# The bias of a transformer block's first FFN product moved out of the weights and into ScalarE's Relu, with a second ScalarE pass over h, and a head worked by pairs of tiles

## Chip, core and metric

The kernel runs on one core of one Trainium2 chip. The metric is the device time of one execution in microseconds (us); the median of several runs counts. The core's engines run side by side, each through its own instructions in order: TensorE (PE in the rows, PEld for its weight loads), VectorE (DVE), ScalarE (ACT), GpSimd (POOL) and SyncE (SP), which issues most transfers. They are kept in step by semaphores: an instruction that waits holds up everything behind it on its engine.

## What is computed

For x of 8 batches x 1024 tokens x 256 channels, in fp32:

```python
xn = (x - mean) / sqrt(var + 1e-5)
q, k, v = split(xn @ qkv_w + qkv_b)            # 16 heads of 16
q, k = l2norm(q), l2norm(k)                    # per head
kv = einsum('bhnd,bhne->bhde', k, v)
attn = einsum('bhnd,bhde->bhne', q, kv) @ proj_w + proj_b
ffn = relu(xn @ W1 + b1) @ W2 + b2             # 256 -> 1024 -> 256
out = x + attn + ffn
```

The last two lines' products are most of the work. b1 is not zero.

## The kernel before

**Precision.** Each operand of a product is split into a high part in fp32r and the rest, a low part; a product is three matmuls (`product`: high x high, high x low, low x high). A high part is a ScalarE copy with rounding, a low part a VectorE (or GpSimd) subtraction of the high part.

**Tiling.** A batch is two halves s (u = 0, 1) of 512 tokens, 4 tiles of 128. W1's 1024 columns are 8 chunks j. `ffn_up(s, u, j)` makes chunk j of W1^T xn^T in PSUM bank `w_bank[j % 2]` with 6 matmuls of 512 columns; `h_high` (ScalarE, L540) writes `h_hi = Relu(w_bank)`; `h_low` (VectorE, L843) writes `h_lo = max(w_bank, 0) - h_hi`; `ffn_down` multiplies both with W2. TensorE's order is written out by hand: `ffn_up` of chunk j + 2, `ffn_down` of chunk j, and between them the query and key products `query_key` (banks `v_bank`, evacuated by `qk_out`, L518 and L475), `gather` (xn^T k into `g_bank`), `key_value`, `project` and, at the end of a batch, `attend`. `ffn_up` of chunk j + 2 waits for `h_lo` of chunk j, since they share a bank. `attend` waits for `m_lo`, the low part of the projected key-value matrix, a VectorE instruction that stands behind `h_low` of the next half's chunk 0 and the norms of the next half's q and k. `gather` waits for `k_lo`. The first `ffn_down` of a half waits for `yT_out` (L555), which empties `o_bank`.

**How the bias of layer 1 gets in.** Channel 0 of xn is raised by 1 for every token (`xn[:, :, 0:1] + 1`). Then xn_raised @ W gives xn @ W + W[0], so each weight matrix gets its bias in row 0's stead by adding (bias - W[0]) to *every row*: that works because a normalised row sums to 0, so that adding the same c to all 256 rows adds c times the raised 1 only. For W1 the row c = b1 - W1[0] is spread over 128 partitions by small fp32 matmuls (`raise_by`, with `raise_signs` made by GpSimd and `raise_rows` cleared by VectorE and loaded by ScalarE's queue), and VectorE adds it to the weights in four parts (`raise_w1`, L769), before `w1_high` and `w1_low` split them. qkv_w is raised in the same way by rows that are loaded spread out.

**The opening.** Half 0 has no predecessor. VectorE takes statistics, `normalise_first` writes the four tiles of xn (L761) and raises channel 0 (L765), TensorE transposes all four (`transpose_x`, 8 transposes), ScalarE and VectorE split each of two banks (`xT_high_first`, `xT_low_first`), and `ffn_up_first` makes chunk 0. The orders of batch 0 and of the first half of batch 1's preparations are written out in `opening` for every engine. In later halves xn^T is made by VectorE's 32x32 transposes and 16 transfers each from SP's queue; q^T too.

**The end.** The last half's result stays token-major. GpSimd adds the output bias to the loaded x (`add_last_bias`, L377) early in batch 7; `bias_out` was loaded and summed in the opening. In the last half `attend(b, 0, w_bank)` waits for the `h_lo` of chunk 7.

Of the kernel before, what the change touches and what calls it, by code (L numbers as in the profile page):

```python
# [62 lines left out]
def build(nc, x, qkv_w, qkv_b, proj_w, proj_b, w1, b1, w2, b2, out):  # L63
# [6 lines left out]
    with ctx:  # L70
# [14 lines left out]

        w1_hi, w1_lo = (sb(f"w1_{n}", [P, KC, INTER], F32R) for n in ("hi", "lo"))
# [21 lines left out]
        h_hi, h_lo = (sb(f"h_{n}", [P, RING, HALF], F32R) for n in ("hi", "lo"))  # L108
        qk_even = sb("qk_even", [P, TILES, 2 * C])
# [22 lines left out]
        bias_ffn = kv[:].rearrange("p g n -> p (g n)")  # L132
# [3 lines left out]
        raise_rows = qk_sq[:].rearrange("p t n -> p (t n)")  # L136
# [15 lines left out]
        w1_raise = [g_bank[:, 0:2 * P], kv_bank[:, 0:2 * P], v_bank[1][:, 0:2 * P], v_bank[1][:, 2 * P:4 * P]]  # L152
# [14 lines left out]
        w1_raise_ready, qkv_raise_ready = sem("w1_raise_ready"), sem("qkv_raise_ready")  # L167
        qkv_rows_loaded = sem("qkv_rows_loaded")
        signs_set, warm_set, raise_rows_cleared = sem("signs_set"), sem("warm_set"), sem("raise_rows_cleared")
        w1_raised, w1_hi_ready, w1_ready = (sem(f"w1_{n}") for n in ("raised", "hi_ready", "lo_ready"))  # L170
# [9 lines left out]
        xn_done, xn_hi_done, xn_split_done = sem("xn_done"), sem("xn_hi_done"), sem("xn_split_done")  # L180
        last_y_set = sem("last_y_set")
# [13 lines left out]
        h_ready, h_done, h_lo_done = (sem(n) for n in ("h_ready", "h_done", "h_lo_done"))  # L195
# [67 lines left out]
        def _(sp):  # L263
# [60 lines left out]
            sp.dma_start(bias_out[:], proj_b.partition_broadcast(P)).then_inc(bias_o_loaded, 16)  # L324
            sp.dma_start(bias_ffn[:], b2.partition_broadcast(P)).then_inc(bias_o_loaded, 16)
# [7 lines left out]
            def half(b, s, u, last):  # L333
# [31 lines left out]
        def _(pool):  # L365
# [37 lines left out]
            nc.gpsimd.memset(raise_signs[:], 0.0).then_inc(signs_set, 1)  # L403
# [637 lines left out]
        def _(pe):  # L1041
# [6 lines left out]
            def tile(t):  # L1048
                return slice(t * P, (t + 1) * P)
# [247 lines left out]
```

## Time and profile before

| | |
|---|---|
| median of 3 runs | 568.85 us (568.74 to 569.23) |
| profiled execution, its own time | 569.29 us |
| its span, first to last instruction | 567.5 us |
| mean granted TensorE clock | 0.998 |
| busy: PE / DVE / ACT / POOL | 559.3 / 414.4 / 282.4 / 119.9 us |
| waits of PE by name (longest) | 1.3 us in all for xn in the head; 0.9 or less each else |

The busy times are those of one execution. A row of the timeline gives start, duration, engine, line, operation, what is written and read, how many instructions, and in brackets how long the engine idled before it and what released it. Matmuls overlap, so a busy PE says little; the distance between the starts of matmuls says more (512 columns: 0.23 us, 256 columns: 0.12 us when nothing waits).

### The profile page before, as it was taken

What the parts mean: (1) busy time and instruction counts of PE and PEld (TensorE: products, weight loads), DVE (VectorE), ACT (ScalarE), POOL (GpSimd) and SP (SyncE); (2) the same over time, 40 slices, a digit from 0 to 9 for tenths busy, and PEclk for the clock granted to TensorE, in tenths of its full rate; (3) what the DMA queues carried; (4) which work ended last, traced back from release to release, by engine and by line L of the source; (5) the groups of instructions that cost most, each with busy time, mean ns of one, the idle gap of its engine ahead of it and who ended that gap; (6) DMA issues with size and microseconds to landing.
All of it is one profiled execution on the core that took longest, in us unless ns stands there. A gap on an engine that the chain in (4) does not pass through costs nothing.

```text
span 567.5 us, 8956 instructions
## 1 busy us (share of the span) xinstructions
PE 559.3 (99%) x2722; PEld 475.5 (84%) x2722; DVE 414.4 (73%) x807; ACT 282.4 (50%) x516; POOL 119.9 (21%) x148
## 2 busy tenths in 40 slices
PE   7999999999999999999999999999999999999997
PEld 6788887888888888888888888888888888888896
DVE  6887887777786767958678585776778767683755
ACT  3586473655435563365634556445554555433421
POOL 2532422502052020520204202231024300150100
PEclk9999999999999999999999999999999999999999
DMA  8322136353523535035451353425444252424423
GB/s 297 112 81 50 29 80 97 81 100 72 101 28 86 95 85 98 16 86 94 85 89 25 85 94 85 81 34 103 76 90 67 43 102 41 82 31 75 110 38 75
DMA packets 141398, 45.36 MB, mean 80 GB/s; under 512 B 133314, under 2 KB 136386, under 8 KB 141380
## 3 DMA queue, kind: packets, MB, share of 16 engines
q1 hardware_dynamic: 139264, 44.61, 39.0%
q10 hardware_dynamic: 2116, 0.53, 0.6%
q8 instruction: 9, 0.15, 0.1%
q14 instruction: 9, 0.07, 0.0%
HBM read 20.98 MB, written 8.39 MB: 52 GB/s over the span
## 4 chain that ended last, share of the span: by engine, by line
PE 89%; SPq 4%; DVE 2%; ACT 2%; issue 1%; DMA 1%; ACTq 0%; DVEq 0%
PE o_bank L1044 11%; PE o_bank L1045 11%; PE o_bank L1046 11%; PE w_bank L1046 10%; PE w_bank L1044 10%; PE w_bank L1045 10%; PE v_bank L1044 6%; PE v_bank L1045 6%; PE v_bank L1046 6%; SPq L308 3%; PE g_bank L1046 3%; PE g_bank L1045 3%; PE g_bank L1044 3%; PE kv_bank L1165 1%; DMA x_sb<-x 1%
## 5 line engine op out<-in xcount | busy, mean ns | idle before, releaser
L843 DVE SCALAR_TENSOR_TENSOR h_lo<-w_bank,h_hi 128x512 fp32r<-128x512 f32 x128 | 87.5, 683 | 34.1 <-ACT h_hi L540 32.6
L540 ACT ACTIVATE h_hi<-w_bank 128x512 fp32r<-128x512 f32 x128 | 76.4, 597 | 70.6 <-PE w_bank L1046 68.8
L1046 PE MATMUL w_bank<-xT_hi,w_lo 128*128 128x512 f32 x254 | 100.0, 394 | 0.0
L1044 PE MATMUL w_bank<-xT_hi,w_hi 128*128 128x512 f32 x254 | 99.7, 393 | 0.0
L1045 PE MATMUL w_bank<-xT_lo,w_hi 128*128 128x512 f32 x254 | 99.7, 393 | 0.0
L1044 PE MATMUL o_bank<-h_hi,w_hi 128*128 128x512 f32 x240 | 95.0, 396 | 0.3 <-ACT wvp_raw L555 0.3
L1045 PE MATMUL o_bank<-h_lo,w_hi 128*128 128x512 f32 x240 | 94.7, 395 | 0.0
L1046 PE MATMUL o_bank<-h_hi,w_lo 128*128 128x512 f32 x240 | 94.6, 394 | 0.0
L372 POOL TENSOR_TENSOR xn_lo<-xn,xn_hi 128x256 fp32r<-128x256 f32 x56 | 41.6, 742 | 224.4 <-ACT xn_hi L475 215.9
L387 POOL TENSOR_TENSOR y_sb<-y_sb,y_rows 128x256 f32<-128x256 f32 x56 | 53.4, 959 | 130.6 <-DVE y_rows L882 108.1
L518 ACT ACTIVATE qk_sq<-v_bank 128x512 f32<-128x512 f32 x64 | 38.4, 599 | 79.0 <-PE v_bank L1046 78.6
L810 DVE TENSOR_REDUCE qk_v<-qk_sq 128x32 f32<-128x512 f32 x64 | 43.4, 680 | 35.6 <-ACT qk_sq L518 35.6
L1046 PEld LDWEIGHTS w_bank<-xT_hi,w_lo 128*128 128x128 f32 x254 | 47.7, 188 | 10.2
L1044 PEld LDWEIGHTS w_bank<-xT_hi,w_hi 128*128 128x128 f32 x254 | 47.7, 188 | 9.6 <-DVE w_lo L702 0.6
L1045 PEld LDWEIGHTS w_bank<-xT_lo,w_hi 128*128 128x128 f32 x254 | 47.7, 188 | 9.4
L1044 PEld LDWEIGHTS o_bank<-h_hi,w_hi 128*128 128x128 f32 x240 | 46.5, 194 | 10.1 <-ACT wvp_raw L555 0.7
L1045 PEld LDWEIGHTS o_bank<-h_lo,w_hi 128*128 128x128 f32 x240 | 46.9, 195 | 9.4
L1046 PEld LDWEIGHTS o_bank<-h_hi,w_lo 128*128 128x128 f32 x240 | 46.7, 195 | 9.2
L1044 PE MATMUL v_bank<-wqk_hi,xT_hi 128*128 128x512 f32 x128 | 50.3, 393 | 0.1
L1045 PE MATMUL v_bank<-wqk_lo,xT_hi 128*128 128x512 f32 x128 | 50.3, 393 | 0.0
L1046 PE MATMUL v_bank<-wqk_hi,xT_lo 128*128 128x512 f32 x128 | 50.1, 391 | 0.0
L493 ACT ACTIVATE xn<-x_sb,ln_offset,ln_rstd 128x256 f32<-128x256 f32 x52 | 27.0, 590 | 29.4 <-DVE ln_offset L754 29.4
(188 smaller groups left out, 986.3 us busy)
## 6 DMA issues: line engine op xcount, KB each, us to landing
qT_lo<-blocks SPq DMA_DIRECT2D x256, 32.0 KB, 1.9
x_sb<-x SPq DMA_DIRECT2D x15, 512.0 KB, 3.9
y_sb<-x SPq DMA_DIRECT2D x60, 128.0 KB, 3.5
out<-y_sb SPq DMA_DIRECT2D x58, 128.0 KB, 2.7
xT_raw<-blocks SPq DMA_DIRECT2D x224, 32.0 KB, 1.9
y_sb<-w SPq DMA_DIRECT2D x4, 256.0 KB, 4.8
w_raw<-w SPq DMA_DIRECT2D x1, 768.0 KB, 8.8
x_sb<-x SPq DMA_DIRECT2D x2, 256.0 KB, 2.9
```

The lines of the kernel that those rows point to most:

```text
L308: sp.dma_start(to_pairs[j * BLOCK:(j + 1) * BLOCK, :, g * run:(g + 1) * run], by_row[g * BLOCK:(g + 1) * BLOCK, j]).then_inc(moved, 16)
L372: nc.gpsimd.tensor_tensor(xn_lo[:, u, t, :], xn_of(s)[:, t, :], xn_hi[:, u, t, :].bitcast(F32), ALU.subtract).then_inc(xn_split_done, 1)
L387: nc.gpsimd.tensor_tensor(y_sb[:, u, t, :], y_sb[:, u, t, :], y_rows[:, u, t, :], ALU.add).then_inc(y_done, 1)
L493: done = nc.scalar.activation(to[:, t, :], x_sb[:, u, t, :], ACT.Identity, bias=ln_offset[:, t:t + 1], scale=ln_rstd[:, t:t + 1])
L518: nc.scalar.activation(qk_sq[:, t % 2, :], v_bank[t % 2][:], ACT.Square).then_inc(qk_sq_done, 1)
L540: nc.scalar.activation(h_hi[:, j % RING, :], w_bank[j % 2][:], ACT.Relu).then_inc(h_done, 1)
L810: nc.vector.tensor_reduce(qk_v[:, t, :], qk_sq[:, t % 2, :].rearrange("p (h d) -> p h d", d=D), AXIS.X, ALU.add).then_inc(qk_ss_done, 1)
L843: nc.vector.scalar_tensor_tensor(h_lo[:, r, :], w_bank[j % 2][:], 0.0, h_hi[:, r, :].bitcast(F32), ALU.max, ALU.subtract).then_inc(h_lo_do ...
L1044: nc.tensor.matmul(to, left[0], right[0], start=first, stop=False, skip_group_check=shared)
L1045: nc.tensor.matmul(to, left[0], right[1], start=False, stop=False, skip_group_check=shared)
L1046: return nc.tensor.matmul(to, left[1], right[0], start=False, stop=last, skip_group_check=shared)
L1165: nc.tensor.matmul(kv_raw[:, g, :, :], wv_hi[:, k, heads], g_parts[:, k, :, heads], start=g == 0 and k == 0, stop=False, skip_group_check= ...
```

## The change

1. W1 is split as loaded: no `raise_by` for W1, no `raise_signs`, no `raise_rows`, no `raise_w1`. xn stays raised by 1 in channel 0. So TensorE's `w_bank` now holds xn @ W1 + W1[0]. With c = W1[0] - b1, h = Relu(w_bank - c).
2. ScalarE's Relu takes the bias `c_up = -c` as a column per partition, and gives `h_hi`. A second ScalarE pass, after a wait for the first, writes `h_g = h_hi + c` (`c_down = c`) in fp32. VectorE then writes `h_lo = max(w_bank, c) - h_g`, which is h - h_hi.
3. c is made once: b1 and W1[0] are loaded as 8 rows of 128, GpSimd subtracts, TensorE transposes to 128x8, ScalarE writes `c_up` and `c_down`.
4. The head: `normalise_first` raises and signals each pair of tiles; `transpose_pair`, `xT_high_pair`, `xT_low_pair` work by pairs (256 columns), `ffn_up_first` now makes chunks 0 and 1, in 24 matmuls of 256 columns. W1's chunk 0 is split first, ahead of ScalarE's square root and VectorE's normalisation.
5. `bias_out` is now loaded and summed in the last batch, into free parts of x_sb: two transfers on SP's queue ahead of `load_y`, one GpSimd addition ahead of `add_last_bias`.

```diff
             def h_high(s, j):
 
+                r = j % RING
+                if is_first(s) and j == 0:
+                    act.wait_ge(c_set, 2)
                 wait(act, h_ready, JC * s + j + 1)
-                nc.scalar.activation(h_hi[:, j % RING, :], w_bank[j % 2][:], ACT.Relu).then_inc(h_done, 1)
+                nc.scalar.activation(h_hi[:, r, :], w_bank[j % 2][:], ACT.Relu, bias=c_up[:, j:j + 1]).then_inc(h_done, 1)
+                wait(act, h_done, JC * s + j + 1)
+                nc.scalar.activation(h_g[:, j % 2, :], h_hi[:, r, :].bitcast(F32), ACT.Identity,
+                                     bias=c_down[:, j:j + 1]).then_inc(h_less_c, 1)
...
             def h_low(s, j):
                 r = j % RING
-                wait(dve, h_done, JC * s + j + 1)
-                nc.vector.scalar_tensor_tensor(h_lo[:, r, :], w_bank[j % 2][:], 0.0, h_hi[:, r, :].bitcast(F32),
-                                               ALU.max, ALU.subtract).then_inc(h_lo_done, 1)
+                wait(dve, h_less_c, JC * s + j + 1)
+                nc.vector.scalar_tensor_tensor(h_lo[:, r, :], w_bank[j % 2][:], c_down[:, j:j + 1],
+                                               h_g[:, j % 2, :], ALU.max, ALU.subtract).then_inc(h_lo_done, 1)
...
@@ ScalarE's opening @@
-            act.wait_ge(raise_rows_cleared, 1)
-            for row, of_w1 in enumerate((b1.rearrange("(o n) -> o n", o=1), w1[0:1, :])):
-                act.dma_start(raise_rows[row:row + 1, :], of_w1).then_inc(rows_loaded, 16)
+            for n, row in enumerate((b1, w1[0:1, :].rearrange("o n -> (o n)"))):
+                act.dma_start(c_rows[:, n, :], row.rearrange("(j p) -> j p", p=P)).then_inc(rows_loaded, 16)
             act.wait_ge(const_set, 2)
             nc.scalar.activation(unread[:], positive[:], ACT.Sqrt)
+            w1_high_first()
             ln_sqrt(0)
-            xT_high_first(0, 0, 0)
             w1_high(0)
-            xT_high_first(0, 0, 1)
+            w1_high(1)
+            xT_high_pair(0, 0)
+            xT_high_pair(0, 1)
+            xT_high_pair(1, 0)
+            xT_high_pair(1, 1)
+            act.wait_ge(c_ready, 1)
+            nc.scalar.activation(c_up[:], c_in_bank, ACT.Identity, scale=-1.0).then_inc(c_set, 1)
+            copy(c_down[:], c_in_bank).then_inc(c_set, 1)
+            w2_high(0)
             h_high(0, 0)
-            w1_high(1)
-            w2_high(0)
...
@@ VectorE's opening @@
-            nc.vector.memset(raise_rows, 0.0).then_inc(raise_rows_cleared, 1)
             variance(0, 0, 0)
+            w1_low_first()
             normalise_first()
-            raise_w1(0)
-            xT_low_first(0, 0, 0)
             w1_low(0)
-            xT_low_first(0, 0, 1)
-            raise_w1(1)
+            for a in range(PAIRS):
+                for k in range(KC):
+                    xT_low_pair(a, k)
+            w1_low(1)
             h_low(0, 0)
-            w1_low(1)
 
             def opening():
                 h_low(0, 1)
-                raise_w1(2)
-                raise_w1(3)
                 w1_low(2)
                 h_low(0, 2)
...
@@ TensorE's opening @@
-            keep_warm(14)
-            pe.wait_ge(signs_set, 3)
-            pe.wait_ge(rows_loaded, 32)
-            raise_by(w1_raise[0], 0).then_inc(w1_raise_ready, 1)
+            keep_warm(13)
+            pe.wait_ge(const_set, 4)
+            pe.wait_ge(c_rows_done, 1)
+            nc.tensor.transpose(c_in_bank, c_rows[:, 0, :], ident[0:JC, 0:JC]).then_inc(c_ready, 1)
             keep_warm(2)
-            pe.wait_ge(const_set, 4)
-            transpose_x(0, 0)
-            raise_by(w1_raise[1], 2 * P).then_inc(w1_raise_ready, 1)
+            transpose_pair(0)
+            transpose_pair(1)
             ffn_up_first()
-            ffn_up(0, 0, 1)
-            raise_by(v_bank[1][:], 4 * P).then_inc(w1_raise_ready, 1)
...
@@ SyncE, a half of a batch @@
+                if last and u == 0:
+                    sp.wait_ge(xn_done, s + 1)
+                    sp.dma_start(bias_out, proj_b.partition_broadcast(P)).then_inc(bias_o_loaded, 16)
+                    sp.dma_start(bias_ffn, b2.partition_broadcast(P)).then_inc(bias_o_loaded, 16)
```

## Rows read from the trace of the kernel before

**Rows 1.** The page's busy times: engine, us, share, instructions.
```profile
PE 559.3 (99%) x2722; PEld 475.5 (84%) x2722; DVE 414.4 (73%) x807; ACT 282.4 (50%) x516; POOL 119.9 (21%) x148
```
**Rows 2.** Windows, one steady batch: stretch, length, busy by engine, PEclk, DMA share, GB/s.
```profile
349.87:418.30 68.43, 68.43 (x327) 58.03 (x327) 50.20 (x100) 35.12 (x65) 13.51 (x16) 1.00 0.40 77
```
**Rows 3.** Groups by shape on ACT, one steady batch: busy us, mean ns, idle before.
```profile
L540 ACT ACTIVATE h_hi<-w_bank 128x512 fp32r<-128x512 f32 x16 | 9.5, 597 | 8.5 <-PE w_bank L1046 8.5
...
L555 ACT ACTIVATE xn_first<-o_bank,bias_T 128x512 f32<-128x512 f32 x2 | 1.4, 688 | 0.2 <-PE o_bank L1046 0.2
```
**Rows 4.** Timeline of ACT, steady batch: a wait on its own result.
```profile
379.01 2.08 ACT L493 ACTIVATE xn<-x_sb,ln_offset,ln_rstd 128x256 f32<-128x256 f32 x4 [2.16 <-DVE ln_offset L754]
381.12 0.21 ACT L497 ACTIVATE xn<-xn 128x4 f32<-128x4 f32 x1
```
**Rows 5.** The chain that ended last, around 28.6 us: start, us, what.
```profile
28.63 0.48 ACT h_hi L540
```
**Rows 6.** Timeline and landing time of W1's first part, the head.
```profile
L270 SPq DMA_DIRECT2D y_sb<-w x1: 434/434/434, 1.7 to 1.7; - x1
...
DMA to landing us min/median/max: 3.8/3.8/3.8
...
7.13 1.38 DVE L761 TENSOR_SCALAR xn<-x_sb,ln_mean,ln_rstd 128x256 f32<-128x256 f32 x4
...
13.00 0.60 ACT L540 ACTIVATE h_hi<-w_bank 128x512 fp32r<-128x512 f32 x1 [1.81 <-PE w_bank L1105]
...
14.97 0.19 PEld L1044 LDWEIGHTS w_bank<-xT_hi,w_hi 128*128 128x128 f32 x1 [0.60 <-DVE w_lo L702]
```
**Rows 7.** Timeline of PEld: query product of tile 2, batch 0.
```profile
30.14 0.20 PEld L1044 LDWEIGHTS v_bank<-wqk_hi,xT_hi 128*128 128x128 f32 x1 [0.35 <-ACT qk_even L475]
```
**Rows 8.** Timelines of DVE and PEld, rest of batch 0, in pairs.
```profile
58.52 0.69 DVE L843 SCALAR_TENSOR_TENSOR h_lo<-w_bank,h_hi 128x512 fp32r<-128x512 f32 x1
...
59.29 0.19 PEld L1044 LDWEIGHTS w_bank<-xT_hi,w_hi 128*128 128x128 f32 x1
...
73.47 0.69 DVE L843 SCALAR_TENSOR_TENSOR h_lo<-w_bank,h_hi 128x512 fp32r<-128x512 f32 x1 [0.27 <-ACT h_hi L540]
...
74.26 0.19 PEld L1044 LDWEIGHTS w_bank<-xT_hi,w_hi 128*128 128x128 f32 x1
...
85.07 0.69 DVE L702 TENSOR_TENSOR m_lo<-g_bank,m_hi 128x512 fp32r<-128x512 f32 x1
...
85.83 0.20 PEld L1044 LDWEIGHTS v_bank<-qT_hi,m_hi 128*128 128x128 f32 x1 [1.26 <-issue]
...
93.34 0.19 PEld L1044 LDWEIGHTS o_bank<-h_hi,w_hi 128*128 128x128 f32 x1 [0.70 <-ACT wvp_raw L555]
```
**Rows 9.** Timelines of DVE and PEld at the end of a steady batch.
```profile
356.16 0.69 DVE L843 SCALAR_TENSOR_TENSOR h_lo<-w_bank,h_hi 128x512 fp32r<-128x512 f32 x1 [0.44 <-ACT h_hi L540]
...
358.72 0.69 DVE L702 TENSOR_TENSOR m_lo<-g_bank,m_hi 128x512 fp32r<-128x512 f32 x1
...
359.99 0.19 PEld L1044 LDWEIGHTS v_bank<-qT_hi,m_hi 128*128 128x128 f32 x1
```
**Rows 10.** Timelines of DVE and PEld in a steady second half.
```profile
402.86 1.21 DVE L702 TENSOR_TENSOR k_lo<-w_raw,k_hi 128x1024 fp32r<-128x1024 f32 x1
...
405.88 0.19 PEld L1044 LDWEIGHTS g_bank<-k_hi,xn_hi 128*128 128x128 f32 x1
```
**Rows 11.** Timelines of POOL, DVE and PEld, last half.
```profile
532.88 2.40 POOL L377 TENSOR_TENSOR y_sb<-y_sb,bias_out 128x1024 f32<-128x1024 f32 x1 [22.67 <-DMA y_sb<-x]
...
533.38 2.98 DVE L829 TENSOR_TENSOR w_raw<-w_raw,qk_rn 128x1024 f32<-128x1024 f32 x1
...
539.93 1.21 DVE L702 TENSOR_TENSOR k_lo<-w_raw,k_hi 128x1024 fp32r<-128x1024 f32 x1
...
541.60 0.19 PEld L1044 LDWEIGHTS g_bank<-k_hi,xn_hi 128*128 128x128 f32 x1
...
554.76 0.20 PEld L1044 LDWEIGHTS w_bank<-qT_hi,m_hi 128*128 128x128 f32 x1 [0.18 <-DVE h_lo L843]
```

More of the change, by code:

```diff
@@ L108, in build @@
         h_hi, h_lo = (sb(f"h_{n}", [P, RING, HALF], F32R) for n in ("hi", "lo"))
+        h_g = sb("h_g", [P, 2, HALF])
         qk_even = sb("qk_even", [P, TILES, 2 * C])
@@ L180, in build @@
         xn_done, xn_hi_done, xn_split_done = sem("xn_done"), sem("xn_hi_done"), sem("xn_split_done")
+        xn_pair_spread, xn_pair_done = sem("xn_pair_spread"), sem("xn_pair_done")
+        xT_pair_ready, xT_pair_hi_done, xT_pair_lo_done = (sem(f"xT_pair_{n}") for n in ("ready", "hi_done", "lo_done"))
         last_y_set = sem("last_y_set")
@@ L566, in w1_high, with w1_high_first @@
             def w1_high(part):
-                cols = part_columns(part)
-                act.wait_ge(w1_raised, part + 1)
+                cols = part_columns(part) if part else chunk_columns(1)
+                act.wait_ge(w1_loaded[part], 16)
                 copy(w1_hi[cols], w1_raw[cols]).then_inc(w1_hi_ready, 1)
+            def w1_high_first():
+                cols = chunk_columns(0)
+                act.wait_ge(w1_loaded[0], 16)
+                copy(w1_hi[cols], w1_raw[cols]).then_inc(w1_first_hi_ready, 1)
             def w2_high(part):
@@ L1054, in of_tile, with transpose_pair @@
                 return columns[:, first:(t // PAIR + 1) * P * PAIR:PAIR]
-            def raise_by(to, first):
-                return nc.tensor.matmul(to, raise_signs[:], raise_rows[:, first:first + to.shape[1]], start=True, stop=True)
+            def transpose_pair(a):
+                if a == 0:
+                    pe.wait_ge(xn_pair_done, 1)
+                else:
+                    pe.wait_ge(xn_done, 1)
+                for k in range(KC):
+                    for e in range(PAIR):
+                        done = nc.tensor.transpose(pair_banks[a][k][:, tile(e)], xn[:, a * PAIR + e, k * P:(k + 1) * P],
+                                                   ident[:])
+                    done.then_inc(xT_pair_ready if a == 0 else xT_ready, 1)
             def transpose_x(s, u):
@@ L1092, in ffn_up, with up_part @@
                 done.then_inc(h_ready, 1)
+            def up_part(j, k, a, weights, of, first=False, last=False):
+                columns = pair_tokens(a)
+                return nc.tensor.matmul(w_bank[j][:, columns], weights[:, k, tile(j)], of[:, 0, k, columns],
+                                        start=first, stop=last, skip_group_check=True)
             def ffn_up_first():
-                pe.wait_ge(w1_hi_ready, 1)
-                for k in range(KC):
-                    pe.wait_ge(xT_hi_done, k + 1)
-                    nc.tensor.matmul(w_bank[0][:], w1_hi[:, k, tile(0)], xT_hi[:, 0, k, :], start=k == 0, stop=False)
-                    if k == 0:
-                        pe.wait_ge(w1_ready, 1)
-                    nc.tensor.matmul(w_bank[0][:], w1_lo[:, k, tile(0)], xT_hi[:, 0, k, :], start=False, stop=False)
```

108 lines of the change are left out of this document (71 added, 37 removed).

## The prediction

> **What bounds the kernel now.** I read the busy times first. TensorE is busy 559.3 of 567.5 us, VectorE 73% of the span, ScalarE 50% [rows 1]. So time is lost only where TensorE waits, and a saving elsewhere is worth nothing unless it ends such a wait. The second view is the table of windows: a steady batch takes 68.43 us and TensorE is busy for all of it, with ScalarE at 35.12 and VectorE at 50.20 [rows 2]. The reader should see two things. In steady batches no wait is left to remove; all that the change can gain lies before TensorE's run of products starts. And ScalarE has 33 us free per batch, so by shares alone an added pass looks free. Whether it is depends on where the free time lies. For that I took the chain of waits and the timelines, and looked for each place where a weight load of TensorE comes close behind the result it waits for. Those places decide, and they are taken one by one below.
>
> **The added pass: its price on each chunk.** There are 128 chunks (8 chunks, 16 halves). Relu with immediates takes 0.60 us; the same shape with a bias column takes 0.69 [rows 3]. A ScalarE instruction that waits for the one before it starts 0.03 after that one's end (379.01 + 2.08 = 381.09, then 381.12) [rows 4]. Without such a wait the next starts before the end: the chain gives a Relu 0.48 before its successor starts [rows 5]. I take 0.69 for `h_g` too: it has the bias column, and reads SBUF.
>
> - Lateness of `h_lo`: before, 0.60 + 0.03 after the Relu starts. After, 0.69 + 0.03 + 0.69 + 0.03 = 1.44. So 0.81 later for each chunk, where VectorE had been waiting.
> - ScalarE's queue: before, the next instruction may start 0.48 after Relu. After, 0.69 + 0.03 for the wait and about 0.60 for the second pass = 1.32. So 0.84 more per chunk, where the queue is full. In all ScalarE gets 128 x (0.69 + 0.09) = 100 us, 282 to 382 us, 67% of the span.
> - `h_lo` itself: same shape, PSUM and SBUF read, a column in place of a constant. No row shows that pair. Below by 0, above by 0.09 (what the column costs ScalarE); I take 0.
>
> **The head.** Gone are four `raise_w1` on VectorE, `raise_by` on TensorE and the clearing of `raise_rows`. The first product of chunk 2 starts at 14.97, released by `w1_low` of part 1, which was queued behind a `raise_w1` [rows 6]. What is late next is `h_lo` of chunk 0. The four normalisations take 1.38 from 7.13 [rows 6]. By pairs, `w1_low_first` and a second addition come between, so the second pair is ready at about 9.0. W1's first part, issued at 1.7, lands 3.8 later, at 5.5 [rows 6], in time for ScalarE: nothing is lost there, but 0.5 more of lateness would delay the square root that is queued behind it. Transposing the second pair ends near 9.6. Then 24 matmuls of 256 columns at 0.12 are 2.9, so chunk 0 is in PSUM at 12.5 instead of 13.0 [rows 6], and chunk 1 soon after. `h_lo` of chunk 0 ends 12.5 + 1.44 + 0.69 = 14.6, and chunk 2 starts at 14.7. The head gains 0.3, not the 1.1 it would gain with the old `h_high`. Bounds 0 and 0.8. The raising of parts 2 and 3 is gone from VectorE's queue too, two additions of 128x512 at about 0.69, but the longer passes of chunks 1 to 3 (0.81 each where they are waited for) use that up: following both queues I find the statistics of half 1, and its normalisation on ScalarE, 0.1 later than before.
>
> **The rest of batch 0.** Here ScalarE has no gaps, and the 0.84 add up. Each line gives how late TensorE gets against the old time.
>
> - Tile 2's query product waits for tile 0's copy, behind chunk 4's Relu [rows 5, 7]. That copy now has the second pass ahead of it: 0.1 + 0.84 = **0.9** late, and the head's 0.3 is swallowed: TensorE only waits longer.
> - Chunk 5's pass adds 0.84 more to ScalarE's queue (1.8, with half 2's normalisation), chunk 6 0.1 to VectorE's (its `h_lo` had been late by transposes anyway), and half 1's chunk 0, right ahead of two evacuations and `xn_high`, 0.2 more: 2.1. `h_lo` of half 1, chunk 2 (58.52, ends 59.21) stood 0.08 ahead of its weight load at 59.29 [rows 8]. So TensorE is **2.1** late.
> - Chunk 3 adds 0.6 to VectorE's queue, which holds the statistics and offsets of half 3. ScalarE normalises 2.8 late, chunk 5 adds 0.81: `h_lo` (73.47, ends 74.16) comes 3.5 late, its weight load was at 74.26, 0.10 behind [rows 8]: **3.5**.
> - Behind chunk 5 ScalarE's queue pushes `qT_high` by another 0.84, VectorE's `qT_low`, the masking of kv and `m_low` (85.07) with it: 4.4 late, and the weight load of `attend` at 85.83 waits for it [rows 8]: **4.4**.
> - The wait at 93.34 came from `xT_high`, fed by SP's moves [rows 8]. Those moves are 2.8 late, TensorE 4.4: the wait goes, 0.4 comes back.
>
> Sum for batch 0: **+4.0**. Bounds: 0.9, if the queues recover behind the first wait; 5.2, if the 0.4 doesn't come back and one more pass counts in full.
>
> **Steady batches.** At the end of a batch VectorE's chain runs without a gap from `h_lo` of the next half's chunk 0 (356.16) to `m_lo` (358.72, ends 359.41); `attend`'s weight load is at 359.99 [rows 9]. Slack 0.58, less 0.05 for the signal. `h_lo` is 0.81 late, so the load waits 0.26. Six batches: **+1.6**, bounds 0 (slack just enough) and 3 (0.5 each). The other places have cover. In a second half VectorE is behind by 1.1 at `k_lo`, which would end at 405.2 instead of 404.1, with `gather`'s load at 405.88 [rows 10]: 0.7 left; if that cover is gone, every 0.1 beyond costs 0.6 us in six batches. The first halves have more.
>
> **The end.** `attend(b, 0, w_bank)` waits for the last `h_lo` with nothing between: its load at 554.76 was already held 0.18 by it [rows 11]. **+0.8**.
>
> GpSimd's addition for the last half ran from 532.88 for 2.40 and a VectorE division beside it took 2.98 [rows 11], against 1.21 for an operation of this shape elsewhere [rows 10]. With two more transfers ahead of the load on SP's queue and one more addition on GpSimd's, the long one starts some 1.5 later and meets the second division instead, which stands in front of `k_lo` (ends 541.14, `gather` loads at 541.60 [rows 11]). Cost between 0 and 1.3 (2.98 less 1.21, less the 0.46 between the last two); I take **+0.3**, since the two must meet for any of it. The Trainium skill's page "SBUF — State Buffer", section "SBUF: two separate sides", says the port pair shared by the two engines is locked for a whole instruction, and the loser waits it out. By that rule a division that starts first loses nothing and the addition waits instead; the row shows a division that started second, so the rule makes 0 as likely as the upper bound.
>
> Costed at nothing: making c (a GpSimd subtraction, a transposition and two 128x8 ScalarE passes), all done while chunk 0's products run until 12.5; if it came later, each 0.1 would hold Relu of chunk 0, and the wait at 30.14 would hide it. The two bias transfers taken from the opening's queue stood behind loads that are needed earlier: 0.
>
> **Sum.** 4.0 + 1.6 + 0.8 + 0.3 = +6.7. The profiled execution took 569.29 (span 567.5 and 1.8 around it); that gives 576.0. The median shown is 0.4 lower, so I predict **575.6**.
>
> **Rivals.**
>
> - *The second pass is hidden, and the head's gain stays.* If `h_g` disappears in ScalarE's free 33 us per batch, the head gives 0.3 to 1.1 and the wait of 0.35 at 30.14 shrinks: about 567.7. For it: the shares [rows 1, 2]. Against: at four loads the result came 0.1 or less ahead or too late [rows 7, 8, 11]. It decides if `h_lo` gets less than 0.1 later. Chance 5%.
> - *No change to be seen:* only the head's gain and the end's 0.8 count, batch 0 recovers. 568.8. Chance 4%.
> - *Half:* the delays of batch 0 do not add up, because queues I count as full have gaps; 1.5 + 0.5 + 0.8 = +2.8, 571.7. Chance 17%.
> - *A further deadline is missed in every second half*, at `k_lo`, or at `yT_out`, which empties `o_bank` behind the new passes. 0.5 to 1 us for 12 halves on top: 582 to 588. Chance 10%.
> - *TensorE's clock falls in the head.* TensorE idles some 2 us between chunk 1 and chunk 2, longer than any pause in the old head, where the granted clock was full. If it fell to 1.2 GHz, a 512-column matmul would take twice its 0.23; for some ten matmuls that is 2.3, half of it hidden by the wait at 30.14: 577. Chance 2%. The Trainium skill's page "TensorE: Matmul & The Clock Gate", section "What's actually happening", tells of such a fall after a pause; the pause it asks for is longer than this one.
> - My own forecast: 62%, by itself 573.5 to 578.5.
>
> **Range and chances.** From the half case at 571.2 to the lower part of the missed deadline at 580.0: that leaves out some 2 in 10. A measurement of this kernel tells 0.2% (1.1 us) from no change. Faster 0.05, same 0.05, slower 0.90.
>
> **What would show it.** `h_g` x128 at 0.69 each and ScalarE near 382 us. Chunk 2's first weight load at 14.7, released by `h_lo`. Waits of TensorE released by ScalarE's copy near 31, by `h_lo` near 61.4 and 77.8, by `m_lo` near 90.3. A steady batch of 68.7 us, with the loss at `attend`. `attend` in the last half held 0.8 longer. The prediction is wrong if the steady batch stays at 68.43, or if `h_g` takes under 0.6; it is wrong in kind if TensorE's start times after 30 us are as before.

## The result, and the profile after

The kernel after takes 579.23 us (median of 5 runs, 578.44 to 581.58) where the kernel before, run beside it, takes 569.23 (568.74 to 569.53): ratio 1.0185, interval 1.017 to 1.0199. It is slower by 10 us. The profiled execution took 578.44 with a span of 576.7. Of the five executions two ran at a granted clock of 1.0 (578.44 and 578.75), three at 0.991 to 0.994 (579.23 to 581.58); why is in the experiments.

The page's busy times of the kernel after, to hold against [rows 1]:

```profile
PE 561.5 (97%) x2727; PEld 476.8 (83%) x2727; DVE 418.1 (72%) x806; ACT 380.9 (66%) x649; POOL 121.0 (21%) x146
```

ScalarE has gained 98.5 us and is still idle for a third of the span. The three groups of the new path, on the page (columns as in [rows 3]):

```profile
L891 DVE SCALAR_TENSOR_TENSOR h_lo<-w_bank,c_down,h_g 128x512 fp32r<-128x512 f32 x128 | 95.4, 745 | 71.3 <-ACT h_g L567 69.8
L565 ACT ACTIVATE h_hi<-w_bank,c_up 128x512 fp32r<-128x512 f32 x128 | 87.6, 685 | 41.7 <-PE w_bank L1091 39.8
...
L567 ACT ACTIVATE h_g<-h_hi,c_down 128x512 f32<-128x512 f32 x128 | 92.7, 724 | 4.2
```

VectorE's `h_lo` now has its idle time ended by `h_g`. Next TensorE's waits, by what ended them (total, times, longest):

```profile
PE w_bank L1089 <- DVE h_lo L891: 6.6, 4, 2.5
PE v_bank L1089 <- issue: 1.7, 1, 1.7
PE v_bank L1089 <- ACT qk_even L487: 1.2, 1, 1.2
...
PE g_bank L1089 <- DVE k_lo L740: 0.8, 1, 0.8
```

Before, the longest wait of TensorE on `h_lo` was 0.2. TensorE's timeline says where they lie:

```profile
14.71 0.47 PE L1089 MATMUL w_bank<-xT_hi,w_hi 128*128 128x512 f32 x1 [2.24 <-DVE h_lo L891]
...
31.18 0.51 PE L1089 MATMUL v_bank<-wqk_hi,xT_hi 128*128 128x512 f32 x1 [1.21 <-ACT qk_even L487]
...
61.71 0.50 PE L1089 MATMUL w_bank<-xT_hi,w_hi 128*128 128x512 f32 x1 [0.98 <-DVE h_lo L891]
...
79.37 0.50 PE L1089 MATMUL w_bank<-xT_hi,w_hi 128*128 128x512 f32 x1 [2.54 <-DVE h_lo L891]
...
91.75 0.48 PE L1089 MATMUL v_bank<-qT_hi,m_hi 128*128 128x512 f32 x1 [1.65 <-issue]
...
550.91 0.36 PE L1089 MATMUL g_bank<-k_hi,xn_hi 128*128 128x256 f32 x1 [0.83 <-DVE k_lo L740]
...
565.05 0.51 PE L1089 MATMUL w_bank<-qT_hi,m_hi 128*128 128x512 f32 x1 [0.86 <-DVE h_lo L891]
```

Five of the seven are in the first 92 us. Setting each of these matmuls against the same one of before gives the ledger (start times; "predicted" adds up the steps of the prediction):

| matmul | before | after | late | predicted |
|---|---|---|---|---|
| chunk 2 of half 0 | 14.98 | 14.71 | -0.27 | -0.3 |
| query of tile 2 | 30.14 | 31.18 | 1.04 | 0.9 |
| half 1, first wait on `h_lo` | 59.52 | 61.71 | 2.19 | 2.1 |
| half 1, second wait on `h_lo` | 74.32 | 79.37 | 5.05 | 3.5 |
| `attend`, batch 0 | 85.86 | 91.75 | 5.89 | 4.4 |
| `attend`, batch 1 | 154.92 | 160.59 | 5.67 | 4.3 |
| `attend`, batch 6 | 497.09 | 505.05 | 7.96 | 5.6 |
| last matmul | 563.30 | 573.61 | 10.31 | 6.7 |
| end of the span | 567.5 | 576.7 | 9.2 | 6.7 |

A steady batch in the windows (columns as in [rows 2]), and the end of the chain to its `attend`:

```profile
367.28:436.12 68.84, 68.80 (x326) 58.14 (x327) 50.77 (x99) 47.24 (x82) 13.59 (x16) 1.00 0.30 76
```
```profile
363.86 0.75 DVE L891 SCALAR_TENSOR_TENSOR h_lo<-w_bank,c_down,h_g 128x512 fp32r<-128x512 f32 x1 [1.30 <-ACT h_g L567]
366.49 0.69 DVE L740 TENSOR_TENSOR m_lo<-g_bank,m_hi 128x512 fp32r<-128x512 f32 x1
```

`m_lo` ends at 367.18 and `attend` starts at 367.28: the 0.58 of slack of [rows 9] is used up. The batch takes 68.84 to 68.93 for 68.43. The distances of starts give 0.29 of it at `attend` (0.20 ahead of its first matmul, 0.09 ahead of the second); the other 0.14 is spread over all 512-column matmuls and no wait goes with it. The DMA share fell from 0.40 to 0.30.

### The profile page after: what moved, and what is told of

Same layout as the page of the kernel before. It is cut to its first block, busy times and chain, and to the rows that moved or that the text cites. A ratio compares the mean times of both kernels' runs of the same rounds, so it can differ in the third digit from the quotient of the medians.

```text
span 576.7 us, 9089 instructions
## 1 busy us (share of the span) xinstructions
PE 561.5 (97%) x2727; PEld 476.8 (83%) x2727; DVE 418.1 (72%) x806; ACT 380.9 (66%) x649; POOL 121.0 (21%) x146
## 3 DMA queue, kind: packets, MB, share of 16 engines
q1 hardware_dynamic: 139264, 44.61, 29.9%
## 4 chain that ended last, share of the span: by engine, by line
PE 84%; DVE 7%; ACT 6%; issue 2%; POOL 1%; DMA 0%; DVEq 0%; ACTq 0%; POOLq 0%
PE o_bank L1090 10%; PE o_bank L1089 10%; PE o_bank L1091 10%; PE w_bank L1089 9%; PE w_bank L1091 9%; PE w_bank L1090 9%; PE v_bank L1089 6%; PE v_bank L1090 6%; PE v_bank L1091 5%; PE g_bank L1089 3%; PE g_bank L1091 3%; PE g_bank L1090 3%; ACT h_g L567 1%; ACT h_hi L565 1%; DVE h_lo L891 1%
## 5 line engine op out<-in xcount | busy, mean ns | idle before, releaser
L891 DVE SCALAR_TENSOR_TENSOR h_lo<-w_bank,c_down,h_g 128x512 fp32r<-128x512 f32 x128 | 95.4, 745 | 71.3 <-ACT h_g L567 69.8
L565 ACT ACTIVATE h_hi<-w_bank,c_up 128x512 fp32r<-128x512 f32 x128 | 87.6, 685 | 41.7 <-PE w_bank L1091 39.8
L567 ACT ACTIVATE h_g<-h_hi,c_down 128x512 f32<-128x512 f32 x128 | 92.7, 724 | 4.2
```

Of the source, the lines that this page charges most:

```text
L565: nc.scalar.activation(h_hi[:, r, :], w_bank[j % 2][:], ACT.Relu, bias=c_up[:, j:j + 1]).then_inc(h_done, 1)
L567: nc.scalar.activation(h_g[:, j % 2, :], h_hi[:, r, :].bitcast(F32), ACT.Identity, bias=c_down[:, j:j + 1]).then_inc(h_less_c, 1)
L891: nc.vector.scalar_tensor_tensor(h_lo[:, r, :], w_bank[j % 2][:], c_down[:, j:j + 1], h_g[:, j % 2, :], ALU.max, ALU.subtract).then_inc(h_ ...
```

## The experiments

All differences are against the kernel after unless said otherwise. The theory: `h_lo` comes one ScalarE pass later, ScalarE's queue grows by as much, and the added time sits where a deadline was tight. Rivals: the new head costs it, or the work on VectorE, or the pace of TensorE itself.

**1. Without the second pass.**

```diff
-                wait(act, h_done, JC * s + j + 1)
-                nc.scalar.activation(h_g[:, j % 2, :], h_hi[:, r, :].bitcast(F32), ACT.Identity, ...)
...
-                                               h_g[:, j % 2, :], ALU.max, ALU.subtract)
+                                               h_hi[:, r, :].bitcast(F32), ALU.max, ALU.subtract)
```

> The changed kernel without the second ScalarE pass; h_lo is max(w_bank, c) - h_hi and so leaves out the subtraction of c. Theory A: the loss is gone and the head's gain shows, 0.997 to 1.001 of the kernel before (567.5 to 569.8), chunk 2 starts near 13.9 us, no wait of TensorE above 0.6 us after 15 us but those of the kernel before and 0.3 or so at the last gather. Theory B: 1.010 or more stays.

570.22 us (569.61 to 571.17), ratio 1.0012, interval 1.0003 to 1.0022, just above the expected 1.001; span 568.4. `attend` of batch 0 starts at 86.27, 5.5 us earlier than after. So the pass is nearly the whole loss: 9.0 of 10 us. The new head without it brings nothing against the kernel before. Chunk 2 starts 1.0 earlier (13.96 for 14.98), but `attend` of batch 0 is 0.4 later than there (86.27 for 85.86), and the pace of the matmuls (below) takes 1.1.

**2. The old head with the pass.** The head and the raised weights of before, with c a column of zeros in Relu, pass and `h_lo`, and the late load of the output bias. Against the kernel before:

```diff
-                nc.scalar.activation(h_hi[:, j % RING, :], w_bank[j % 2][:], ACT.Relu).then_inc(h_done, 1)
+                nc.scalar.activation(h_hi[:, r, :], w_bank[j % 2][:], ACT.Relu, bias=c_up[:, j:j + 1]).then_inc(h_done, 1)
+                wait(act, h_done, JC * s + j + 1)
+                nc.scalar.activation(h_g[:, j % 2, :], h_hi[:, r, :].bitcast(F32), ACT.Identity,
+                                     bias=c_down[:, j:j + 1]).then_inc(h_less_c, 1)
```

> The kernel before, with its W1 raised as before and its old head, plus the second ScalarE pass with columns of zeros (h_lo waits for it) and the late load of the output bias. Theory A (the second pass makes the whole loss, through ScalarE's queue and the later h_lo): 1.015 to 1.022 of the kernel before, that is as slow as the changed kernel or up to 1.5 us slower, with the same waits at the query product of tile 2 and at up(4) and up(7) of half 1, the attend of each batch and the gather of the last half. Theory B (the new head by pairs or the unraised W1 disturbs batch 0, the pass alone costs only the wait at attend and the end): 1.003 to 1.007.

582.08 us (581.71 to 582.26), ratio 1.0214, interval 1.0197 to 1.0231. The loss is there without the new head, and 2.9 us larger, where the expectation had up to 1.5: with the pass, chunk 2 starts at 15.96 here for 14.71 after, and further waits on `h_lo` come near 22 and 29 us. All four executions have a granted clock of 0.997; less the 1.6 that this costs (below), and against the two of after at 1.0, some 2 us stay. So the head by pairs does seem to pay, but only against the cost that comes with it. This trace also showed something new. TensorE after its longest wait:

```profile
82.72 0.50 PE L1056 MATMUL w_bank<-xT_hi,w_hi 128*128 128x512 f32 x1 [2.54 <-DVE h_lo L855]
83.05 0.39 PE L1057 MATMUL w_bank<-xT_lo,w_hi 128*128 128x512 f32 x1
...
84.00 0.63 PE L1058 MATMUL w_bank<-xT_hi,w_lo 128*128 128x512 f32 x1
84.43 0.63 PE L1056 MATMUL o_bank<-h_hi,w_hi 128*128 128x512 f32 x1
84.85 0.63 PE L1057 MATMUL o_bank<-h_lo,w_hi 128*128 128x512 f32 x1
```

And the windows of the same stretch:

```profile
84.00:85.00 1.00, 1.00 (x4) 0.81 (x3) 0.75 (x1) 1.00 (x3) 0.00 (x0) 0.50 0.22 55
85.00:86.00 1.00, 1.00 (x4) 0.81 (x3) 0.74 (x1) 1.00 (x3) 0.00 (x0) 0.50 0.19 44
86.00:87.00 1.00, 1.00 (x4) 0.72 (x4) 1.00 (x3) 0.97 (x3) 0.00 (x0) 0.50 0.26 63
```

The starts go from 0.23 apart to 0.43, and the granted clock is 0.50, that is 1.2 GHz. Here it fell while TensorE was already working again, some 1.2 us behind the end of a wait of 2.54; in numbers 5 and 8 it stood at 0.50 before the wait of 2.5 at the same place was over. Eight matmuls at 0.20 more each are 1.6 us.

**3. The pass runs, but nobody waits for it.** c is left out of `h_lo`; the pass stays in ScalarE's queue.

```diff
-                wait(dve, h_less_c, JC * s + j + 1)
+                wait(dve, h_done, JC * s + j + 1)
...
-                                               h_g[:, j % 2, :], ALU.max, ALU.subtract)
+                                               h_hi[:, r, :].bitcast(F32), ALU.max, ALU.subtract)
```

> The changed kernel with the second pass issued as now, but h_lo takes h_hi and waits for h_hi alone; leaves out the subtraction of c. ScalarE's queue keeps its added 0.84 us per chunk, the 0.76 us of the path to h_lo are gone. Theory A says that both count in batch 0 and only the path counts at each attend and at the end: steady batches back to 68.4 to 68.6 us, in batch 0 a wait of about 1 us at the query product of tile 2 and a late up(7) remain, total 1.004 to 1.010. If the queue were harmless (rival), 1.000 to 1.002; if the queue were all, 1.014 or more.

575.11 us (573.51 to 575.59), ratio 1.0097, interval 1.008 to 1.0114, about half the loss: 4.9 above number 1, where the queue alone is longer, and 4.1 below the kernel after, where `h_lo` waits too. The wait at tile 2's query is there in full (1.20 for 1.21), the 2.5 near 79 is gone, the steady batch is 68.57. So both count: the queue and the longer path to `h_lo`.

**4. No pass in batch 0.** `h_high` returns before the pass in halves 0 and 1, and `h_low` reads `h_hi` there.

```diff
+                if is_first(s) or is_second(s):
+                    return
                 wait(act, h_done, JC * s + j + 1)
                 nc.scalar.activation(h_g[:, j % 2, :], h_hi[:, r, :].bitcast(F32), ACT.Identity,
```

> The changed kernel without the second pass in halves 0 and 1 (leaves out the subtraction of c from h_lo there); all later halves keep it. Theory A: batch 0 gives its 5 to 5.9 us back, steady batches keep their 0.3 at attend, the end its 0.9 and 1.0: 1.006 to 1.009 of the kernel before. Rival (steady batches carry the most): above 1.012.

573.68 us (573.03 to 573.96), ratio 1.0074, interval 1.0059 to 1.009: 5.5 less than after. The steady batches are as after:

```profile
294.10:362.94 68.84, 68.80 (x326) 58.13 (x327) 50.75 (x99) 47.24 (x82) 13.57 (x16) 1.00 0.30 77
```

The two times split the loss: 5.5 of 10 us lie in the one batch that is opened by hand.

**5. Tile 0's copy ahead of chunk 4's pass**, to remove the wait at 31 us.

```diff
                 w2_high(3)
+                qk_out(0, 0, 0)
                 normalise(1, 1)
                 h_high(0, 4)
-                qk_out(0, 0, 0)
                 qk_out(0, 0, 1)
```

> The changed kernel with ScalarE's evacuation of the first query product moved ahead of the normalisation of half 1. The wait of 1.52 us at the query product of tile 2 falls to 0.5 or less in either case. Theory A (batch 0 is one chain through ScalarE's and VectorE's queues up to attend near 91.75; the waits of TensorE only show how far ahead it is): the wait comes back at up(4) and up(7) of half 1, attend starts at 91.2 to 92.0, total within 0.5 us of the changed kernel. Rival (the waits add up one by one): attend near 90.7, total 1.0 to 1.2 us below.

579.99 us (579.36 to 581.35), ratio 1.0191, interval 1.0175 to 1.0207: nothing won. `attend` of batch 0 starts at 93.50 in this profile, later than either theory had it; W1's first part landed late there (see number 8) and the clock stood at 0.50 from 80 to 83.4 us. The wait at the query was gone and stood elsewhere:

```profile
42.88 0.50 PE L1089 MATMUL w_bank<-xT_hi,w_hi 128*128 128x512 f32 x1 [0.60 <-DVE h_lo L891]
...
62.54 0.50 PE L1089 MATMUL w_bank<-xT_hi,w_hi 128*128 128x512 f32 x1 [1.22 <-DVE h_lo L891]
```

**6. The same move in the kernel before,** the same two lines of diff.

> The kernel before with the evacuation of the first query product ahead of the normalisation of half 1. Theory A (batch 0's chain decides): the wait of 0.43 us at 30.14 goes and comes back at attend (85.86): same, 0.999 to 1.001. Rival (waits add up): 0.4 us or 0.0007 faster, hardly told apart in time but visible in the trace as attend at 85.4.

569.36 us (569.10 to 570.10), ratio 1.0003, interval 0.9993 to 1.0013. Its wait at 30.1 went, and 0.46 came at 60.01; `attend` of batch 0 starts at 86.62, 0.76 later than before, and the total is the same. In batch 0 of either kernel a single wait is worth nothing: the lateness is that of ScalarE's and VectorE's queues, and TensorE only meets it in one place or another.

**7. The correction on VectorE.** No ScalarE pass; `h_g = max(w_bank, c) - h_hi`, then `h_lo = h_g - c`, both on VectorE.

```diff
-                nc.scalar.activation(h_g[:, j % 2, :], h_hi[:, r, :].bitcast(F32), ACT.Identity, ...)
...
+                nc.vector.scalar_tensor_tensor(h_g[:, j % 2, :], w_bank[j % 2][:], c_down[:, j:j + 1],
+                                               h_hi[:, r, :].bitcast(F32), ALU.max, ALU.subtract).then_inc(h_less_c, 1)
...
+                nc.vector.tensor_scalar(h_lo[:, r, :], h_g[:, j % 2, :], c_down[:, j:j + 1], None,
+                                        ALU.subtract).then_inc(h_lo_done, 1)
```

> The changed kernel with the subtraction of c moved to VectorE: h_g = max(w_bank, c) - h_hi into fp32, then h_lo = h_g - c; no second ScalarE pass. Path to h_lo about 0.5 us longer than before the change in place of 0.87, VectorE's queue 0.4 to 0.7 longer per chunk. Theory A expects ScalarE's waits to go and VectorE's chain in batch 0 to carry the loss instead: 1.005 to 1.015. If only ScalarE's queue matters: under 1.004.

588.53 us (587.01 to 591.71), ratio 1.0331, interval 1.0287 to 1.0375: far above the 1.015 of the expectation, which had the cost in batch 0 alone. VectorE is busy 82% of the span and a steady batch takes 70.0, with 1.15 lost ahead of `gather` in each, released by `k_lo`. The 0.7 of cover that the prediction found at [rows 10] is real: 16 more passes of 0.54 on VectorE's queue use it up, the second ScalarE pass did not.

**8. The two bias transfers earlier** on SP's queue, ahead of the stores of batch 6.

```diff
+                if last and u == 0:
+                    sp.wait_ge(xn_done, s + 1)
+                    sp.dma_start(bias_out, proj_b.partition_broadcast(P)).then_inc(bias_o_loaded, 16)
+                    sp.dma_start(bias_ffn, b2.partition_broadcast(P)).then_inc(bias_o_loaded, 16)
                 if u == 0:
                     for stored_half in range(2):
                         store_y(b - 1, stored_half)
```

> The changed kernel with the two transfers of the output bias issued before the moves of q at the start of the last batch, so that nothing new stands in front of the last loads. The wait of 0.99 us at the last gather was put down to GpSimd's long addition starting just ahead of VectorE's division (division 3.42 us). Theory A: the addition starts about 1.0 us earlier against VectorE, the division takes 2.4 to 2.9, the wait at gather falls to 0 to 0.5; total 0.5 to 1.0 us below the changed kernel (1.016 to 1.018). Rival (the wait is that of the later h_lo alone, contention is no matter): unchanged, the wait stays at 0.9 to 1.0.

580.17 us (577.69 to 581.01), ratio 1.0175, interval 1.0155 to 1.0194: no difference in the time that can be told. In the trace there is one. The kernel after, GpSimd and VectorE in the last half:

```profile
542.39 2.39 POOL L391 TENSOR_TENSOR y_sb<-y_sb,x_sb 128x1024 f32<-128x1024 f32 x1 [2.71 <-DMA y_sb<-x]
...
542.44 3.42 DVE L877 TENSOR_TENSOR w_raw<-w_raw,qk_rn 128x1024 f32<-128x1024 f32 x1
```

and here:

```profile
547.22 1.22 DVE L877 TENSOR_TENSOR w_raw<-w_raw,qk_rn 128x1024 f32<-128x1024 f32 x1
549.01 1.22 DVE L877 TENSOR_TENSOR w_raw<-w_raw,qk_rn 128x1024 f32<-128x1024 f32 x1
```

With the addition out of the way (543.30 to 545.71) both divisions take 1.22, not the 2.4 to 2.9 of the expectation, and the last `gather` waits 0.31 in place of 0.99. In the other traces with the late transfers the first division starts ahead of the addition. Number 9:

```profile
542.80 1.22 DVE L877 TENSOR_TENSOR w_raw<-w_raw,qk_rn 128x1024 f32<-128x1024 f32 x1
543.33 2.95 POOL L391 TENSOR_TENSOR y_sb<-y_sb,x_sb 128x1024 f32<-128x1024 f32 x1 [2.54 <-DMA y_sb<-x]
545.48 1.89 DVE L877 TENSOR_TENSOR w_raw<-w_raw,qk_rn 128x1024 f32<-128x1024 f32 x1
```

The division that started first takes its 1.22, the addition becomes 0.56 longer, and the second division, which starts behind it, is held to 1.89. `gather` waits some 0.35 in these traces where `h_lo` waits for the pass. So the collision costs 0.7 in the profile of after, and next to nothing in others.

The profile of this number shows another cost of the new head. ScalarE's first split of W1 waits for the transfer, and the square root of half 0 stands behind it in the queue. After, then number 8:

```profile
4.96 0.42 ACT L487 ACTIVATE w_hi<-y_sb 128x256 fp32r<-128x256 f32 x1 [1.70 <-DMA y_sb<-w]
6.00 0.20 ACT L491 ACTIVATE ln_sd<-ln_v 128x4 f32<-128x4 f32 x1 [0.62 <-DVE ln_v L784]
```
```profile
6.01 0.42 ACT L487 ACTIVATE w_hi<-y_sb 128x256 fp32r<-128x256 f32 x1 [2.75 <-DMA y_sb<-w]
6.34 0.19 ACT L491 ACTIVATE ln_sd<-ln_v 128x4 f32<-128x4 f32 x1
```

In the nine profiles with the new head this split starts between 4.96 and 7.13, in five of them (numbers 4, 5, 7, 8 and 9) at 5.95 or later, and everything behind it is late by as much as the square root is. With the old head the first split comes at 10 us, and chunk 2 starts between 14.87 and 15.13 in all four profiles without the pass. Here the clock fell in the head as well, and chunk 2 starts at 16.79:

```profile
10.00:11.00 1.00, 1.00 (x6) 1.00 (x6) 0.77 (x3) 0.73 (x3) 0.00 (x0) 0.50 1.03 382
```

**9. TensorE's waits filled** with dummy products (5 ahead of chunk 2, 6 behind `key_value` in half 1, ahead of the wait near 79 us).

```diff
+            for _ in range(5):
+                nc.tensor.matmul(v_bank[0][:, 0:P], ident[:], ident[:], start=True, stop=True)
...
                         key_value(b)
+                        if is_second(s):
+                            for _ in range(6):
+                                nc.tensor.matmul(g_bank[:, 0:P], ident[:], ident[:], start=True, stop=True)
```

> The changed kernel with small matmuls that nobody reads in its two longest waits of TensorE: 5 after the first products, 6 after key_value of half 1 (about 2 us each). In four of five executions of the changed kernel the mean clock was below 1.0 and the time 0.3 to 3 us above the fastest. Theory C (TensorE's pauses of over 2 us let its clock fall in some executions): all executions at a mean clock of 0.998 or more, the median 0.5 to 1 us below the changed kernel, near 578.4, the spread of executions under 1 us. Rival (the clock's falls have nothing to do with these waits): clocks and spread as before, time the same or 0.2 us more.

578.71 us (577.88 to 579.15), ratio 1.0164, interval 1.015 to 1.0178. All five executions have a granted clock of 0.999 or 1.0, where three of after's five had 0.991 to 0.994. The stretch that ran at 1.2 GHz in number 2, here:

```profile
79.00:82.00 3.00, 2.14 (x9) 1.82 (x10) 1.98 (x3) 2.97 (x7) 1.84 (x3) 1.00 0.21 51
```

The fall costs about 1.6 us where it comes behind the wait near 79, and it belongs to the spread, not to the loss: the two executions of after at a clock of 1.0 take 578.44 and 578.75. That the waits bring it about fits numbers 2, 5, 8 and this one, but is not shown. Against after the median is only 0.5 lower, with overlapping intervals, and the five here still spread over 1.3 us at a full clock, more than the 1 expected; the landing of W1 (number 8) can do that. (After had three executions of five below 1.0, not the four of the expectation.) And there are falls that these two waits do not explain: the clock is at 0.50 in the head of numbers 7 and 8, ahead of chunk 2, and six of ten executions of number 1 and four of number 11 have 0.997, though neither has a wait on `h_lo` above 1.5 in its profile.

**10. The kernel before once more**, unchanged, for the 0.14 per batch.

> The kernel before, unchanged, for a trace taken beside the experiments' ones. In the first trace a steady batch takes 68.43 us; in all traces with the new columns 68.57 and, with the pass awaited, 68.87. If the 0.14 belongs to the chip and not to the change, this trace has 68.5 to 68.6 as well; if the change makes it (the wider h_lo), 68.43.

569.32 us in one run, and a steady batch of 68.43 again. The pace belongs to the kernels, not to the chip of the day.

**11 and 12. One column each.** Number 11 is number 1 with the constant 0 in `h_lo`; number 12 is the kernel before with a column of zeros in `h_lo`, declared ahead of `x_sb`:

```diff
         head_mask = sb("head_mask", [P, KC, P])
+        c_down = sb("c_down", [P, JC])
...
-                nc.vector.scalar_tensor_tensor(h_lo[:, r, :], w_bank[j % 2][:], 0.0, h_hi[:, r, :].bitcast(F32),
+                nc.vector.scalar_tensor_tensor(h_lo[:, r, :], w_bank[j % 2][:], c_down[:, j:j + 1], h_hi[:, r, :].bitcast(F32),
```

> The kernel after without the second pass and with the constant 0 in place of the column in h_lo = max(w_bank, 0) - h_hi; c is added in Relu alone (c is left out of h_lo, so the low part is not that of the reference). Only ScalarE's Relu reads a column. The kernel after and the one without the second pass both ran their matmuls at 68.57 us per steady batch where the kernel before takes 68.43. If ScalarE's bias column costs that, it is 68.57 here too, and the time is 570.2. If VectorE's column costs it, the steady batch is 68.43 and the time about 569.3.

> The kernel before, with its old head, Relu without a bias and no second pass, but with h_lo = max(w_bank, column) - h_hi, the column being zero (same output as before). If VectorE's column costs 0.14 us per batch, the steady batch is 68.57 and the time 570.3, and h_lo lasts 745 ns where it lasted 683. If the pace comes from ScalarE's bias column, the steady batch is 68.43 and the time 569.4; h_lo at 745 ns may then still cost something in the last half, 0.1 at most.

Number 11: 569.73 us (568.79 to 571.43), ratio 1.0012, interval 1.0002 to 1.0022. Number 12: 573.75 us (573.59 to 574.25), ratio 1.0085, interval 1.0068 to 1.0102. Windows of a steady batch, first of 11, then of 12:

```profile
292.88:361.45 68.57, 68.57 (x327) 58.22 (x326) 50.09 (x100) 36.54 (x66) 13.50 (x16) 1.00 0.31 77
```
```profile
293.65:362.70 69.05, 69.05 (x327) 58.16 (x326) 51.05 (x100) 35.10 (x65) 13.55 (x16) 1.00 0.42 76
```

Both theories are wrong. One column alone goes with 0.14, the other alone with 0.62, and both together (number 1) with 0.14. `h_lo` is the same in numbers 1 and 12 (742 and 743 ns), so reading the columns does not explain the pace. No wait goes with it: in number 12 TensorE is busy for all 69.05. What else differs is where the buffers lie. Each of the two 128x8 columns takes 32 bytes of every partition and pushes all that is declared behind it; everything else that the change adds or removes there is a multiple of 512 bytes. The kernels of this study fall into three layouts: no shift (before, 6 and 10) 68.43; 32 bytes (12) 69.05; 64 bytes (after and 1, 3, 4 and 11) 68.57 between waits. The pages' lines of the main DMA queue fall into groups too; the kernel before, then after, then number 12:

```profile
q1 hardware_dynamic: 139264, 44.61, 39.0%
```
```profile
q1 hardware_dynamic: 139264, 44.61, 29.9%
...
out<-y_sb SPq DMA_DIRECT2D x58, 128.0 KB, 2.1
```
```profile
q1 hardware_dynamic: 139264, 44.61, 40.0%
```

The same 139264 packets take a quarter less engine time at 64 bytes than at 0 or 32 (29.3% to 30.5% in all kernels with 64, 38.9% to 40.0% in the others), and a store lands in 2.1 or 2.2 us instead of 2.7 or 2.8. Layout fits all twelve runs, and neither the columns nor the new head does (number 2 has the old head and 29.7%); but no run moved buffers alone, and that shifts by multiples of 512 bytes do no harm is taken for granted. So it is argued, not shown.

## Why the prediction was right, and where its sum was off

The direction, the mechanism and the places were right; 579.23 lies in the range of 571.2 to 580.0 and 0.7 above the likeliest case's own. The sum was +6.7, the profile shows +9.2; the median is another 0.8 above the profiled execution. There is luck in the range: the last stores gave 1.1 back for a reason that the prediction did not have, and without it the median would lie at 580.3, outside.

- **Price of a pass.** Predicted 0.69 for `h_g` and ScalarE near 382 us; measured 0.724 and 380.9. `h_lo` was taken as unchanged, bounds 0 and 0.09; it takes 0.745 for 0.683, 0.06 more.
- **Head.** Right in this profile: -0.3 predicted, -0.27 measured, released by `h_lo`, and swallowed at 31 us. The remark that a later W1 would delay the square root was no side matter: it came true in five of nine profiles (number 8), and no term of the sum has it.
- **Batch 0, first two steps.** Right: 0.9 and 2.1 predicted, 1.04 and 2.19 measured.
- **Batch 0, third step: the term that was mis-sized.** "Chunk 3 adds 0.6 to VectorE's queue, ... ScalarE normalises 2.8 late" gave 3.5; it is 5.05, and the normalisation is 4.26 late (69.53 to 73.79). The cause stands in VectorE's timeline, the statistics of half 3, first before, then after:

```profile
64.68 0.16 DVE L742 TENSOR_SCALAR ln_m<-ln_m 128x4 f32<-128x4 f32 x1
...
65.36 0.16 DVE L746 TENSOR_TENSOR ln_v<-ln_m,ln_dif 128x4 f32<-128x4 f32 x1
```
```profile
67.14 0.63 POOL L457 CAST wv_hi<-wvp_raw 128x512 fp32r<-128x512 f32 x1
67.85 1.29 POOL L459 TENSOR_TENSOR wv_lo<-wvp_raw,wv_hi 128x512 fp32r<-128x512 f32 x1
...
67.90 1.27 DVE L780 TENSOR_SCALAR ln_m<-ln_m 128x4 f32<-128x4 f32 x1
...
69.27 0.46 DVE L784 TENSOR_TENSOR ln_v<-ln_m,ln_dif 128x4 f32<-128x4 f32 x1
```

  An operation on 4 columns takes 1.27 instead of 0.16, because it now starts just behind a GpSimd subtraction of 1.29 and ends with it. The statistics begin 3.08 late (61.99 to 65.07) and end 4.2 late (65.52 to 69.73): 1.1 us that no queue count contains. The same 1.27 is in the traces of numbers 2, 5, 8 and 9, and it is 0.15 in number 1. The next step, 0.9 to `attend`, is right in size (5.05 to 5.89).
- **The 0.4 that comes back** at 93.34: right; the wait is gone, and from `attend` of batch 0 to that of batch 1 the lateness falls by 0.22 (predicted 0.14).
- **Steady batches.** The wait at `attend` is right: 0.26 predicted (its own rows give 0.81 less 0.53, which is 0.28), 0.29 measured. Missing was the pace, 0.14 a batch.
- **The end.** +0.8 predicted, 0.90 measured (1.03 for 0.13).
- **The last gather.** +0.3 predicted, 0.99 in this profile. The prediction had the addition start 1.5 later and meet the second division. Against `attend` of batch 6 it is 1.55 later, but the divisions are 1.1 later too; in this execution it met the first, 0.05 ahead of it. The Trainium skill's page "SBUF — State Buffer", section "SBUF: two separate sides", has the loser wait out the whole instruction. The trace agrees: the addition ends at 544.78 and the division 1.08 later, and in [rows 11] it is 535.28 and 536.36, again 1.08; in number 9, where the division starts first, it is the addition that takes longer. The prediction's reading of the row, a partial slowdown, was the weaker one.
- **What neither side of the sum had:** from the start of the last matmul to the end of the span it is 3.1 us in place of 4.2, as the last stores land sooner. That gives 1.1 back.
- **Rivals.** "Hidden" fell with numbers 1 and 2. "Half" is refuted by the first batch's 5.89. "A further deadline in every second half" did not come: no steady `gather` waits. The clock's fall was looked for in the head at 2%. In the profile of after a wait of 2.24 left it at 1.0; in those of numbers 7 and 8 it did fall in the head, around the wait for xn and not between chunks 1 and 2; in those of numbers 2, 5 and 8 it fell around the wait near 80 us, which the prediction did not consider. The Trainium skill's page "TensorE: Matmul & The Clock Gate", section "What's actually happening", asks for a longer pause than any that TensorE had here; number 2 shows the fall all the same, so the measurement decides.

In the miss of 2.5: +1.5 to `attend` of batch 0 (1.1 of it the statistics), +0.9 in the steady batches (0.7 to 0.8 of it the pace), +1.2 in the last batch (0.7 the gather), -1.1 at the end. What stays open is the byte layout: which buffer's place sets the pace of the matmuls and which that of the transfers.

## What to carry to other kernels

An engine that is idle for half of the time is not free work space: ask how close each of its results comes before the one that waits for it, and where the queue has no gap; here a pass of 0.72 us cost nothing in 15 of 16 places of a steady batch and 5.5 us in the opening. When a queue is made late, add what its instructions will now run beside, not only how long the queue is. And before a few tenths of a per cent are put down to an operation, hold the pace of TensorE between waits against that of the kernel before: it moved by 0.9% in a kernel that only declared and read one column of 32 bytes more. Last, a split put first in a queue makes all behind it wait for its transfer; look at more than one execution before calling that transfer in time.

## What the runs showed of the hardware

- TensorE's granted clock fell to 0.50 (1.2 GHz) in a stretch that began some 1.2 us behind a wait of 2.54 us (number 2), and inside waits of 2.54 and 2.58 at the same place (numbers 5 and 8). It does not do so in every execution: a wait of the same length left it at 1.0 in the profile of after, and so did 2.24 in the head. In the head it fell around a wait for xn of 1.23 (number 8) and 2.46 (number 7), and did not around one of 2.43 (number 4).
- A VectorE operation of 128x4 took 1.27 us instead of 0.16 beside a GpSimd subtraction; a division of 128x1024 took 3.42 instead of 1.22. Where the division started first it took 1.22, and the GpSimd addition 2.95 instead of 2.39 (number 9).
- A column in place of a constant costs VectorE's `scalar_tensor_tensor` 0.06 us at 128x512 (683 to 743 ns in number 12), as it costs ScalarE 0.09 ([rows 3], 597 to 685).
- In number 12, where the buffers behind the new column lie 32 bytes further, 512-column matmuls went 0.9% slower with no wait (68.43 to 69.05 a batch). In the kernels with 64 bytes they went 0.2% slower, while the transfers' share of the DMA engines fell from 39.0% to 29.9% and a store of 128 KB landed in 2.1 or 2.2 us for 2.7. That the place of the buffers is the cause is argued only.
